# Row maxima in pieces of up to 1024 columns over two PSUM banks in a fused attention kernel

## The reference, cut to what matters

```
scores = einsum('bhqd,bhkd->bhqk', Q, K)
scores = where(causal_mask, NEG_INF, scores) * scale
attn = softmax(scores, axis=-1)
ctx = einsum('bhqk,bhkd->bhqd', attn, V)
```

## Time and profile before

| | us |
|---|---|
| median of three runs | 2805.51 |
| lowest and highest | 2802.87, 2821.97 |
| the profiled execution | 2802.04 |
| its span | 2800.0 |
| TensorE busy | 2531.5 |
| VectorE busy | 2177.0 |
| ScalarE busy | 1724.4 |
| GpSimd busy | 692.9 |
| mean granted TensorE clock | 0.946 of full speed |

### The profile page before, as it was taken

How to read it: one execution, slowest core, us unless ns; L and a number is a source line. 1 busy time by engine, 2 the same in 40 slices (tenths; PEclk the granted TensorE clock), 3 DMA queues, 4 the chain that set the end, 5 groups by cost and what they waited for, 6 DMA issues and landing times. The chain is left out here.

```text
span 2800.0 us, 49359 instructions
## 1 busy us (share of the span) xinstructions
PE 2531.5 (90%) x16192; PEld 1296.4 (46%) x16192; DVE 2177.0 (78%) x5272; ACT 1724.4 (62%) x3477; POOL 692.9 (25%) x715
## 2 busy tenths in 40 slices
PE   6988999999999999999999999999996589999990
PEld 5871333333333333333333333333332479999990
DVE  6979888888888888888888888888822867777761
ACT  3660377777666666666666666666674257777760
POOL 2444332100010101011010110101001435556553
PEclk8995799999999999999999999999998689999995
DMA  4989778602404134040431504224013535555548
GB/s 145 317 300 276 282 279 298 192 12 71 96 28 98 49 78 119 15 114 30 95 99 31 120 28 97 62 68 105 19 49 117 186 82 91 86 92 92 90 70 253
DMA packets 217599, 331.29 MB, mean 118 GB/s; under 512 B 27024, under 2 KB 157584, under 8 KB 217360
## 3 DMA queue, kind: packets, MB, share of 16 engines
q1 hardware_dynamic: 137728, 170.68, 21.3%
q0 software_dynamic: 58512, 136.67, 19.2%
q10 hardware_dynamic: 21120, 20.97, 2.4%
HBM read 140.23 MB, written 187.20 MB: 117 GB/s over the span
## 5 line engine op out<-in xcount | busy, mean ns | idle before, releaser
L1023 ACT ACTIVATE probs<-ps 128x512 f32<-128x512 f32 (+3 forms) x2400 | 1121.2, 538 | 653.7 <-PE ps L1318 343.0
L1047 DVE TENSOR_REDUCE early<-ps 128x1 f32<-128x512 f32 x1536 | 1001.7, 684 | 108.2 <-PE ps L1235 101.7
L1235 PE MATMUL ps<-kh,qs 96*128 96x512 bf16 (+3 forms) x2560 | 890.8, 364 | 78.2 <-DVE early L1047 29.9
L1318 PE MATMUL ps<-qs,kh 99*128 99x512 bf16 (+3 forms) x2560 | 827.5, 350 | 16.5 <-ACT probs L1023 7.1
L1334 PE MATMUL ps<-probs,vs 128*32 128x512 f32 (+3 forms) x5120 | 602.3, 542 | 0.0
L1235 PEld LDWEIGHTS ps<-kh,qs 96*128 96x128 bf16 x2560 | 249.5, 99 | 698.5 <-DVE early L1047 313.4
L1043 DVE CUSTOM_DVE_ANT_0 junk<-ps,causal 128x128 bf16<-128x128 f32 (+3 forms) x1024 | 480.1, 483 | 49.0 <-PE ps L1235 44.8
L1318 PEld LDWEIGHTS ps<-qs,kh 99*128 99x128 bf16 x2560 | 245.5, 98 | 287.1 <-ACT probs L1023 135.2
L1735 POOL DMA_INDIRECT acc<-y,to x156 | 251.9, 1615 | 117.8 <-ACT y L1790 72.5
L951 POOL DMA_INDIRECT rows_out<-row,place_a x96 | 95.2, 992 | 716.2 <-DVE place_a L726 669.7
L1322 PE MATMUL ps<-ident_b,causal_b 128*128 128x128 bf16 x1024 | 213.8, 220 | 0.0
(11 more groups left out here) (230 smaller groups left out, 2997.1 us busy)
## 6 DMA issues: line engine op xcount, KB each, us to landing
rows_out<-row POOLq DMA_DIRECT2D x129, 544.0 KB, 3.6
xg<-rows_out SPq DMA_DIRECT2D x39, 544.0 KB, 3.8
v_ones<-vt SPq DMA_DIRECT2D x16, 1024.0 KB, 6.3
vs<-v_ones SPq DMA_DIRECT2D x16, 1024.0 KB, 11.5
contexts<-ctx_out SPq DMA_DIRECT2D x64, 256.0 KB
q_parts<-parts SPq DMA_DIRECT2D x32, 384.0 KB, 4.6
k_parts<-parts SPq DMA_DIRECT2D x32, 384.0 KB, 4.5
qs<-q_parts SPq DMA_DIRECT2D x64, 192.0 KB, 7.7
```

The lines of the kernel that those rows point to most:

```text
L1023: nc.scalar.activation(probs[u % PB][:, h, q0:TB], bank(s % SB)[:, q0:TB], ACT.Exp, scale=SCALE).then_inc(exp_done, 1)
L1047: nc.vector.tensor_reduce(early[:, h, t, k0 // CW:k0 // CW + 1], tile, AX.X, ALU.max).then_inc(max_done, 1)
L1235: nc.tensor.matmul(tile[:, 0:w], qh[a % HR][0:STACK, t * P:(t + 1) * P], kh[a % HR][0:STACK, k0:k0 + w], start=True, stop=True).then_inc(m ...
L1318: mm = nc.tensor.matmul(tile[:, q0:TB], kh[a % HR][:, kt * P:(kt + 1) * P], qh[a % HR][:, j * TB + q0:(j + 1) * TB], start=True, stop=not ...
```

## The change

`CW` becomes 1024, and a piece over 512 columns takes two neighbouring banks: TensorE fills them with two matmuls, and VectorE reduces both with one instruction. A group then has 96 pieces instead of 160: a query tile up to number 7 is one piece (the custom instruction alone, up to 1024 wide), and tiles 8 to 15 have one early piece of 1024 and a last one of 128 to 1024. The number of matmuls stays at 160 a group, and so do their columns. For tiles 9 and 11 the last piece comes before the early one, so that two pieces of one bank each stand side by side.

`psum_banks` gives out the four banks piece by piece: a cursor goes round, a wide piece starts on an even bank (and skips one where it must), and for each bank of a piece `FREED_BY` names the use that had it last. TensorE waits for that use before it writes the bank, in `take` for the first and in `max_chunk` for the second. `early` has one column a row, so `early_max` and its reduction go. All positions of side work are given anew in numbers of wide pieces.

```diff
-CW = 512
+CW, BANK = 1024, 512
-    for h in range(HG) for t in range(QT) for k0 in range(0, P * (t + 1), CW)
+    for h in range(HG) for t in range(QT) for k0 in range(0, P * (t + 1), CW)[::-1 if t in (9, 11) else 1]
...
-WIDEN, MOD, GATE_INVERSE, FIRST_PLACES = 20, (30, 34, 38, 42), (60, 80, 100, 120), 140
-INVERT, CONTEXT, PROJECT, RESIDUAL, STATISTICS, DEVIATION = 64, 50, (56, 60), (66, 70), 75, 79
-CENTRE, MODULATE, TRANSPOSE, ROUTE, PROBABILITY, RANK = 84, 90, (97, 101), 110, 120, 123
-SHARE, COUNT, OVER = 126, 136, 146
+WIDEN, MOD, GATE_INVERSE, FIRST_PLACES = 13, (19, 21, 23, 26), (37, 48, 61, 72), 85
+INVERT, CONTEXT, PROJECT, RESIDUAL, STATISTICS, DEVIATION = 40, 31, (35, 37), (41, 43), 46, 48
+CENTRE, MODULATE, TRANSPOSE, ROUTE, PROBABILITY, RANK = 51, 55, (59, 62), 67, 73, 75
+SHARE, COUNT, OVER = 77, 83, 89
...
+def psum_banks():
+
+    at, before, last, cursor = [], [], [None] * MS, 0
+    for slot, (kind, g, k) in enumerate(STREAM):
+        n = 2 if kind == "chunk" and CHUNKS[k][3] > BANK else 1
+        cursor += cursor % n
+        first = cursor % MS
+        at.append(first)
+        before.append(last[first:first + n])
+        last[first:first + n] = [slot] * n
+        cursor = first + n
+    return at, before
+
+
+FIRST_BANK, FREED_BY = psum_banks()
...
-            return bank(4 + SLOT[kind, g, k] % MS)
+            wide = kind == "chunk" and CHUNKS[k][3] > BANK
+            return bank(4 + FIRST_BANK[SLOT[kind, g, k]], 2 if wide else 1)
...
-                        nc.vector.tensor_reduce(early[:, h, t, k0 // CW:k0 // CW + 1], tile, AX.X, ALU.max
+                        nc.vector.tensor_reduce(early[:, h, t:t + 1], tile, AX.X, ALU.max
                                                 ).then_inc(max_done, 1)
...
-                    nc.vector.tensor_reduce(early_max[:, :, :], early[:, :, :, :], AX.X, ALU.max
-                                            ).then_inc(max_all, 1)
-                    dve.wait_ge(max_all, 2 * g + 1)
-                    nc.vector.tensor_tensor(maxima[p][:, :, :], maxima[p][:, :, :], early_max[:, :, :], ALU.max
+                    nc.vector.tensor_tensor(maxima[p][:, :, :], maxima[p][:, :, :], early[:, :, :], ALU.max
...
-                    if slot >= MS:
-                        pe.wait_ge(*freed(slot - MS))
-                    return bank(4 + slot % MS)
+                    if FREED_BY[slot][0] is not None:
+                        pe.wait_ge(*freed(FREED_BY[slot][0]))
+                    return slot_bank(kind, g, k)
...
-                    nc.tensor.matmul(tile[:, 0:w], qh[a % HR][0:STACK, t * P:(t + 1) * P],
-                                     kh[a % HR][0:STACK, k0:k0 + w], start=True, stop=True).then_inc(max_mm, 1)
+                    for n, k1 in enumerate(range(0, w, BANK)):
+                        if n and FREED_BY[SLOT["chunk", g, c]][n] is not None:
+                            pe.wait_ge(*freed(FREED_BY[SLOT["chunk", g, c]][n]))
+                        k2 = min(k1 + BANK, w)
+                        mm = nc.tensor.matmul(tile[:, k1:k2], qh[a % HR][0:STACK, t * P:(t + 1) * P],
+                                              kh[a % HR][0:STACK, k0 + k1:k0 + k2], start=True, stop=True)
+                    mm.then_inc(max_mm, 1)
```

More of the change, by code:

```diff
@@ L745, in attend @@
         maxima = [sb(f"maxima{p}", [P, HG, QT]) for p in range(2)]
-        early = sb("early", [P, HG, QT, (S - 1) // CW])
-        early_max = sb("early_max", [P, HG, QT])
+        early = sb("early", [P, HG, QT])
         neg = [sb(f"neg{p}", [HG * QT, PARTS, P], BF16) for p in range(2)]
@@ L1029, in _ @@
                 dve.wait_ge(tables_set, 2)
-                nc.vector.memset(early[:, :, :, :], -3e38).then_inc(mask_set, 1)
+                nc.vector.memset(early[:, :, :], -3e38).then_inc(mask_set, 1)
                 dve.wait_ge(mask_set, 1)
@@ L1234, in max_chunk @@
                     tile = take("chunk", g, c)
-                    nc.tensor.matmul(tile[:, 0:w], qh[a % HR][0:STACK, t * P:(t + 1) * P],
-                                     kh[a % HR][0:STACK, k0:k0 + w], start=True, stop=True).then_inc(max_mm, 1)
+                    for n, k1 in enumerate(range(0, w, BANK)):
[5 more added lines that the diff above has]
+                    mm.then_inc(max_mm, 1)
                 def max_turn(g):
-                    pe.wait_ge(max_all, 2 * (g + 1))
+                    pe.wait_ge(max_all, g + 1)
                     nc.tensor.transpose(take("turn", g, 0)[0:HG * QT, 0:P],
```

## The result

The changed kernel takes 2930.3 us in the median of four runs (2926.5 to 2932.8) against 2805.6 for the kernel before: a ratio of 1.0436, 95% interval 1.0406 to 1.0465. The forecast was 2823 with a range from 2762 to 2862: the likeliest case had the direction and not the size, 4.4% slower instead of 0.6%.

The account below looks back on a forecast made before the run. TensorE was taken to bound the plain groups, VectorE some 27 us of a mixed period. Plain +4, mixed +16.5, start -2 and turn -1 on 2802.0 us gave 2819.5; with 3.5 for the median, 2823 us, range 2762 to 2862.

Parts of the forecast that it names:

- Who bounds what: TensorE bounds plain groups (attention and maxima only), at most 3 us to win; VectorE paces some 27 us of mixed periods.
- the rival that VectorE bounds all of it: VectorE sets the pace throughout, so its saving counts everywhere: 74 us faster, 2732 us; chance 0.03.
- the one of a dearer reduction: A reduction over two banks costs clearly over 1.22 us, 1.4 say: 6 us a group, 2880 us; chance 0.02.
- Coarser buffer: At VectorE's bursts its allowed lateness falls from 1.6 to 0.9 us: 2.1 us lost a mixed period, bounds 0 and 4.2.
- The rival that the coarse buffer decides: Wide pieces wait for whole pairs at every burst and side tile: +64 us, 2870 us; chance 0.18.
- my sign for refuting the step: Mixed periods' bank wait after the ranking: 2.4 instead of 1.75 us would confirm the buffer step, under 1.5 refute it.
- Fewer reductions: On VectorE, 64 pieces a group go, saving some 4.6 us; worth nothing where TensorE paces, 1.0 us a mixed period.
- The rival that the saving is paid out: VectorE's saving counts in full in the mixed groups: 53 us faster, 2753 us; chance 0.17.
- Side tiles in a pair: A one-bank side tile makes the next wide piece skip its neighbour: 0.4 us more a mixed period, bounds 0 and 2.
- Uneven scores: Two matmuls at one point crowd scores elsewhere: 1 us a group, bounds 0 and 2; in mixed periods absorbed by existing stalls.
- The start: Before 300 us VectorE is saturated: 4.6 us pure gain, about half lost refilling pairs; -2 us, bounds -4.6 and 0.
- Side work renumbered, at nothing: Side work keeps about its place in columns, with no VectorE work added and no DMA moved: nothing, covered by TensorE.

Follow-up runs that it names:

- The chain's last step: From the changed kernel with each wide piece reduced by two instructions (2957.7 us) to one reduction, the change itself: span -33.1 us.
- the largest memset: The kernel before with a 192-column VectorE memset behind each of 64 early reductions a group: 2888.5 us, ratio 1.0294.
- The chain's second row: From the kernel before with both 512-column matmuls at one point (2836.9 us) to banks in pairs, still two reductions (2957.7 us): span +126.2 us.
- the order alone: The kernel before, with both 512-column pieces of each 1024 at one point, own banks and reductions kept: 2836.9 us, ratio 1.0110.

## Why the prediction was wrong, step by step

**Who bounds what: held in the plain groups.** The chain's last step takes 4.6 us of work from VectorE in a plain period (89.73 to 85.15) and gives 1.1; the largest memset adds 9.6 and costs 1.9. I had said nothing, and it is a fifth to a quarter; the rival that VectorE bounds all of it is out. So is the one of a dearer reduction, at 1220 ns.

**Coarser buffer: the step that failed.** I had it at 2.1 us a mixed period and at nothing in a plain one, and so the periods at 119 to 122.5 and 103.5 to 106; they are 128.7 on average and 107.5 in three of the four. The chain's second row measures 3.9 a plain and 8.8 a mixed period. No token block's side work runs in the plain ones. The mixed one also holds dearer side tiles and the later root (both below), and how much of it is the buffer alone no run tells; one bank of four less, with neither of them changed, costs 7.9. The mechanism was the right one and was priced as if only long bursts could meet it. Two things were wrong in the formula (1.6 us of lateness allowed before, 0.9 after). First, 1.6 was too high. In the trace of before VectorE works 1.22 us on something else, and TensorE, which should start its next piece 0.22 after a score, starts 0.75 after it, 0.53 lost. The bank that it waits for is that of the piece begun at 1309.14, four uses earlier, which VectorE reduces only at 1311.17:

```profile
1309.14 0.38 PE L1235 MATMUL ps<-kh,qs 96*128 96x512 bf16 x1
...
1310.04 1.22 DVE L1155 TENSOR_TENSOR work<-work,gate_inv 128x1024 f32<-128x1024 f32 x1
...
1311.16 0.38 PE L1318 MATMUL ps<-qs,kh 99*128 99x512 bf16 x1
1311.17 0.68 DVE L1047 TENSOR_REDUCE early<-ps 128x1 f32<-128x512 f32 x1
...
1311.91 0.39 PE L1235 MATMUL ps<-kh,qs 96*128 96x512 bf16 x1 [0.36 <-DVE early L1047]
```

So a burst may take about 0.7 us here (1.22 less 0.53) before TensorE stands still, not 1.6. The 1.6 came from the 2.8 us in which a full unit goes once round the four banks, as if the pieces arrived evenly and VectorE were never behind. Here the bank is wanted again after 2.24 us (1311.38 less 1309.14), which leaves 1.0 by the same formula; and the piece had landed at 1309.52, so VectorE was 0.5 behind before the burst began. Second, the change takes 0.7 us from the allowance by my own figure, so hardly anything is left, and TensorE waits at ordinary unevenness. The plain period after shows it on TensorE; the same stretch of before has no recorded wait for VectorE at all, and 0.2 us for ScalarE:

```profile
699.31 0.27 PE L1253 MATMUL ps<-kh,qs 96*128 96x256 bf16 x1
700.09 0.60 PE L1253 MATMUL ps<-kh,qs 96*128 96x512 bf16 x2 [0.51 <-DVE early L1064]
```

No side work stands here. My condition for being wrong, stalls of over 0.5 us outside bursts, is met in this row. It is the only recorded wait for VectorE in the period, though, and TensorE's recorded waits there are 1.3 us of the 3.8 lost; that the rest lies under the modelled tails is argued from the length of the period, not seen. The rival that the coarse buffer decides had the direction, its 5.2 us a mixed and 2 us a plain period being still too little; my slip was to give it 0.18. The Trainium skill, page "Perfetto Trace Analysis", section "Optimization Strategy", says that the same gap repeating on the engine that should be saturated can mean too few PSUM buffers; the time of the three-bank run agrees, with 5.0 us a plain and 7.9 a mixed period for one bank of four.

At the bursts the step was near. At the ranking TensorE starts a piece's first matmul at 1356.53 and its second at 1358.73: 1.98 lost (2.20 less 0.22), where 2.4 were forecast and 1.75 stood before; my sign for refuting the step was under 1.5. A wait of the same size has appeared at the centring; here are TensorE's rows, and then VectorE's of the same time:

```profile
1319.41 0.38 PE L1253 MATMUL ps<-kh,qs 96*128 96x512 bf16 x1
1321.44 0.28 PE L1253 MATMUL ps<-kh,qs 96*128 96x256 bf16 x1 [1.64 <-DVE maxima L1060]
```
```profile
1319.10 1.67 DVE L1148 SCALAR_TENSOR_TENSOR work<-work,mv_b,mod_rows 128x256 f32<-128x256 f32 x4
1320.69 0.68 DVE L1060 CUSTOM_DVE_ANT_0 junk<-ps,causal 128x512 bf16<-128x512 f32 x1
```

Both rows of TensorE are of one wide piece. Its first bank is free and its second is held by the 512-wide piece that VectorE reaches only behind the centring. VectorE waits for both halves, so the first bank is held unread meanwhile, TensorE's queue stands, and VectorE gets the piece late.

**Fewer reductions: the instruction was right, its worth was not.** The last row of the chain gives 33 us, 27 by the medians and 19 by the ratios, and in a mixed period 2.3 where I had 1.0. The rival that the saving is paid out, 53 us, was thus a third to three fifths true by itself, and was overrun by the pairs. This worth is measured on a kernel that already stalls at its pairs, not on the kernel before. VectorE's work counts not only in the 27 us in which it was plainly the bound; I take it that less work also gives banks back sooner wherever TensorE is about to want one, but no run tests that.

**Side tiles in a pair: under-priced.** TensorE's recorded waits for ScalarE's copies (the transposes' and the route tile's) were 2.6 us in 11 periods. After, for the one and for the other copy:

```profile
PE ps L1253: 9.4, 11
```
```profile
PE ps L1253: 8.6, 11
```

That is 15.4 us more, 1.4 a mixed period against 0.4 forecast, inside its bounds. With single tiles and four banks the order alone waits 2.7 and 6.1 us for the same copies, and the three-bank kernel 12.6 and 7.3. So some 6 us of the 15.4 come with the order, and waits as long as these arise without any skipped neighbour.

**Uneven scores: about right where they were counted,** 1.2 us a plain period against 1.0. In the mixed ones I let stalls that were there anyway take them up; the order costs 2.5 each instead, of which 0.6 are the waits for the copies just named.

**The start: the wrong sign.** The pure gain was there, -4.1 us, but I took half of it as the price of refilling a pair, and it was 10.7. VectorE, never idle before but for one 4.1 us wait, waited for TensorE 21 times from 213 to 307 us, 11.9 us in all, of which the longest, 3.7, stands where the 4.1 did. Its groups of waits (us, times, longest), and the timeline of one such place:

```profile
DVE early L1064 <- PE ps L1253: 7.2, 16, 0.7
DVE junk L1060 <- PE ps L1253: 4.7, 5, 3.7
```
```profile
242.40 1.23 DVE L1064 TENSOR_REDUCE early<-ps 128x1 f32<-128x1024 f32 x1
243.54 0.28 DVE L1060 CUSTOM_DVE_ANT_0 junk<-ps,causal 128x128 bf16<-128x128 f32 x1
243.68 1.89 PE L1253 MATMUL ps<-kh,qs 96*128 96x512 bf16 x4 [0.78 <-DVE early L1064]
243.75 0.42 DVE L1060 CUSTOM_DVE_ANT_0 junk<-ps,causal 128x256 bf16<-128x256 f32 x1
244.82 2.36 DVE L1064 TENSOR_REDUCE early<-ps 128x1 f32<-128x1024 f32 x2 [0.65 <-PE ps L1253]
```

The granted clock is 0.50 here. TensorE can refill the pair only from 243.68, when the wide reduction ends, and VectorE has just a 128- and a 256-wide piece to do meanwhile. My sum compared a refill with another wide reduction (2.4 against 2.26 us); the neighbour is often a narrow one.

**"Side work renumbered, at nothing": wrong by way of ScalarE,** which the prediction left out of this term. VectorE now waits for the root that ScalarE makes between two table loads, and TensorE for an exponential held up by them. ScalarE's rows, VectorE's and TensorE's, of one period after:

```profile
1323.07 1.20 ACT L1040 ACTIVATE probs<-ps 128x512 f32<-128x512 f32 x2 [2.53 <-PE ps L1337]
1324.29 1.28 ACT L998 ACT_TABLE_LOAD   x1
1325.58 0.20 ACT L998 ACTIVATE rstd_b<-rstd_b 128x4 f32<-128x4 f32 x1
1325.80 1.28 ACT L1040 ACT_TABLE_LOAD   x1
1327.10 2.06 ACT L1040 ACTIVATE probs<-ps 128x512 f32<-128x512 f32 x4
```
```profile
1325.82 0.18 DVE L1154 RECIPROCAL rstd_b<-rstd_b 128x4 f32<-128x4 f32 x1 [1.15 <-ACT rstd_b L998]
```
```profile
1325.87 0.38 PE L1337 MATMUL ps<-qs,kh 99*128 99x512 bf16 x1
1327.75 0.39 PE L1337 MATMUL ps<-qs,kh 99*128 99x512 bf16 x1 [1.50 <-ACT probs L1040]
```

ScalarE had itself waited 2.53 us for TensorE's scores, which the centring had held up. One late bank thus goes round: TensorE, ScalarE, VectorE, TensorE. Issuing the root two scores earlier gave 25 us back. How much of this is the renumbering is open: by the tables of the two kernels the root stands one score later in a group than before (76 instead of 75), with the modulation at 77 in both, and the three-bank kernel, with the root unmoved, waits for it too, 5.7 us in 11 mixed periods against 14.0.

**What of the four-percent loss is clock, is only argued.** The granted clock over the mixed periods was 1.00 before and is 0.96 after. Two windows of 6 us, at the centring's stall and just behind the one for the exponential, show 1.00 and 0.72; in the second TensorE runs in part at the lower of its levels, 1.2 GHz:

```profile
1319.00:1325.00 6.00, 4.36 (x30) 1.32 (x28) 5.10 (x14) 3.45 (x7) 0.00 (x0) 1.00 0.01 3
1329.00:1335.00 6.00, 5.48 (x27) 2.13 (x27) 2.82 (x7) 2.41 (x5) 0.00 (x0) 0.72 0.00 0
```

The plain periods after the first lose their 4 us with the clock at 1.00, and with three banks the mixed periods are 7.9 us longer at 0.99, so the clock adds to the stalls and isn't the cause of them. Its size can be estimated from the mixed periods after: the four at 0.99 take 126.6 to 127.9 us, the five at 0.95 take 129.7 or 129.8. If all eleven had been like the first kind, some 17 of the 99 us would not be there; whether the clock made them longer or longer stalls lowered the clock, these rows can't tell.

## What to carry to other kernels

Price a buffer by the longest wait of the trace that it hides now, read at a place where the reader really was late, and not by its mean spacing; banks that are taken and given back in pairs, with all that came with them, cost here about as much as one bank of four less, and four to six times what the merged reductions saved. A matmul stream that is busy 99.8% has no slack of its own, so a wait on it lengthens the stage; where the engines that it feeds have fixed work of their own, as ScalarE's root had here, part of it is paid again.

## What the runs showed of the hardware

One VectorE reduction over two PSUM banks (1024 fp32 columns) has no surcharge: 1220 ns alone, 1.14 us behind another. A memset of 4, 56 or 192 columns queued behind a reduction is recorded with 62, 105 and 218 ns and costs 12, 28 and 150 (the first to within some 6 ns): the recorded times of these short VectorE instructions can't be summed.
